# One fused attention and mixture-of-experts kernel: the routing arithmetic and the shared expert reordered at the seam between its two halves

## Chip, core and metric

The kernel runs on one core of a Trainium2 chip (trn2). Its time is device time in microseconds, the median over runs. Five engines work side by side, each in its own program order: PE (TensorE) multiplies matrices, DVE (VectorE) and ACT (ScalarE) do elementwise work, POOL (GpSimd) does elementwise work and issues indirect DMAs, and SP (SyncE) issues the plain DMAs. They meet only at semaphores that the program sets and waits for.

## What is computed

A layer in two halves, on 2048 tokens of width 512. The first half is cross attention with 16 heads whose queries, keys, values and probabilities are rounded to 8 bits. The second is a mixture of experts:

```python
logits = flat @ router_w.T                        # flat: layernorm of x, 2048 x 512; 32 experts
scores = sqrt(softplus(logits))
_, idx = top_k(scores + expert_bias, 4)
topv = take_along_axis(scores, idx, axis=1)
topv = topv / (topv.sum(-1, keepdims=True) + 1e-20)
out = sum over experts of p[:, None] * clamped_swiglu(flat, wg, wu, wd)   # p is topv, zero elsewhere
out = out + clamped_swiglu(flat, shared_gate_w, shared_up_w, shared_down_w)
return x + out                                    # x already holds the attention's result
```

`clamped_swiglu` clips both products to -7..7, takes `silu(g) * u` (256 wide) and multiplies by the down weights. The shared expert serves every token; a routed expert serves only those tokens that chose it.

## The kernel before

Tokens go in 16 tiles of 128 (`TT = 16`, numbered from 0), heads in 16 units a tile, so attention has 256 units (`LAST` is unit 255). A unit's scores go from PSUM to SBUF on DVE, through the exponential on ACT, through a DMA transpose on SP, are widened from uint8 to bf16 on POOL (`probs_ready`) and are multiplied by the values on PE (`av_done`). When all units of a tile are done, DVE normalises it (`an`, L643 and L648), PE projects it, and `x1`, `xn2` (its layernorm) and the router's logits follow. `LAG = 7` is the distance in units at which PE follows. Unit 254 is an exception: DVE widens it (`widen`, L1104 to L1109), so that POOL has only unit 255 left.

The seam is what comes after unit 255 and before the first routed tile. Each engine has a program for it: `pe_early`, `act_early`, `dve_early`, `pool_early` and `sp_early`. All but the last begin with a loop over `l` in 0..31, which plays out the last steps of the attention with the seam's work put at chosen values of `l`. Three chains run there.

- **Routing** (mostly DVE). `soft_first` and `soft_last` make the softplus with ACT's Exp and Ln; ACT's Sqrt gives the scores; `choose_first` and `choose_last` find the best four and write one-hot masks (`maskb`, `r_mask`); `pe_ranks` counts by matmuls how many earlier tokens chose each expert (`r_totals`); from that DVE works out each token's slot (`base`, `slotf`, `slot_n`) and builds, for each of the four choices `j`, the operands of a matmul that makes the token list: `name_of(j, 0)`, `name_of(j, 1)` and `place_of(j)`. PE multiplies them (`pe_list(j)`, `listed`). After the fourth DVE writes `rows_sb` (`rows_ready`), and POOL gathers the first tokens with it. The routing is done for tiles 0 to 12 first (`TA = 13`, the slice `most`), then for tiles 13 to 15 (`rest`).
- **Shares.** The normalised weight of each chosen expert is written to DRAM beside the token (`share_ready`, then one DMA on SP).
- **Shared expert**, 16 tiles. ACT does Silu (`act_silu`), DVE multiplies (`hidden(k)`, L926, `h_ready`), PE transposes (`pe_hidden`), ACT evacuates (`act_hidden`), PE does the down product (`pe_down`), ACT evacuates into one of four buffers `y` (`act_early_out`), and POOL adds it to the output with an indirect DMA (`add`, L1309), whose landing frees the buffer. Gate and up products of tiles 0 to 12 (`GATED = 13`) were made during the attention and lie in DRAM; four buffers `xg` take them back. SP loads them (`tokens(k)`, which waits until `hidden(k - 4)` has freed the buffer), and tile 4 to 12 are clamped on POOL (L1369), in program order ahead of `add(k - 6)`. `gate(k)` clamps tiles 13, 14 and 15 out of PSUM on DVE; `pe_up` makes them.

SP also loads the first five routed experts (`load_expert`, two pieces of 768 KB each; `FREE_RING = 5`) while the shared expert runs: both pieces of expert 0 right after `tokens(8)`, of expert 1 after `tokens(9)`, and so on to `tokens(12)`; then it stores the shares. Experts 5, 6 and 7 are loaded when `listed` says that the list is made.

The routed stage follows: 78 tiles, each with gathers on POOL and two products and a transpose on PE. It is not touched by the change.

## Time and profile before

| | us |
|---|---|
| median of 3 runs | 1362.32 |
| lowest and highest run | 1361.37 and 1363.89 |
| the profiled execution's own time | 1359.23 |
| its span (first to last instruction) | 1357.5 |
| PE busy in the span | 1189.9 |
| DVE busy in the span | 1106.5 |
| attention's last exponential starts (from the span's start) | 819.31 |
| first gather of routed tokens is issued | 907.64 |
| first product of the routed stage | 917.6 |

Times below count from the start of the span. A row of the timeline gives start, duration, engine, line, operation, output and input, shape and count, and in brackets how long the engine had been idle before it and what released it. Several instructions of one line are merged into one row.

### The profile page before, as it was taken

What the parts mean: (1) busy time and instruction counts of PE and PEld (TensorE: products, weight loads), DVE (VectorE), ACT (ScalarE), POOL (GpSimd) and SP (SyncE); (2) the same over time, 40 slices, a digit from 0 to 9 for tenths busy, and PEclk for the clock granted to TensorE, in tenths of its full rate; (3) what the DMA queues carried; (4) which work ended last, traced back from release to release, by engine and by line L of the source; (5) the groups of instructions that cost most, each with busy time, mean ns of one, the idle gap of its engine ahead of it and who ended that gap; (6) DMA issues with size and microseconds to landing.
All of it is one profiled execution on the core that took longest, in us unless ns stands there. A gap on an engine that the chain in (4) does not pass through costs nothing.

```text
span 1357.5 us, 29324 instructions
## 1 busy us (share of the span) xinstructions
PE 1189.9 (88%) x7425; PEld 594.4 (44%) x7523; DVE 1106.5 (82%) x2287; ACT 938.2 (69%) x1345; POOL 886.3 (65%) x905
## 2 busy tenths in 40 slices
PE   7999577888888889888888886759999999999995
PEld 3444134444444455444444443324444444444442
DVE  4557899999999999999999998865767767766663
ACT  2224398999999999999999996424555555555552
POOL 3222388998889898989889985374445445445443
PEclk9999789999999999999999997989999999999997
DMA  7565877787777677776767794896778887786542
GB/s 264 134 155 132 162 133 159 138 162 139 143 148 154 141 148 142 148 150 144 151 138 146 143 211 100 269 219 180 159 207 224 221 231 190 182 236 176 91 69 26
DMA packets 400754, 219.32 MB, mean 162 GB/s; under 512 B 357287, under 2 KB 357415, under 8 KB 400690
## 3 DMA queue, kind: packets, MB, share of 16 engines
q1 hardware_dynamic: 380354, 179.72, 55.4%
q0 software_dynamic: 20336, 38.83, 16.0%
q8 instruction: 29, 0.48, 0.1%
q14 instruction: 35, 0.29, 0.1%
HBM read 101.10 MB, written 40.89 MB: 105 GB/s over the span
## 4 chain that ended last, share of the span: by engine, by line
PE 49%; issue 18%; DVE 17%; POOL 5%; ACT 5%; DMA 4%; SPq 1%; DVEq 0%; POOLq 0%; ACTq 0%; another core or an unknown queue 0%
PE psS L1417 20%; PE psS L885 10%; DVE mem L638 6%; DVE mem L654 6%; PE psS L477 4%; POOL mem L728 3%; ACT mem L595 3%; PE psS L1864 3%; DMA mem<-mem 2%; PE psAV L1851 2%; PE psP L864 1%; PE psAV L528 1%; PE psP L427 1%; POOL mem L711 1%; PE psAV L448 1%
## 5 line engine op out<-in xcount | busy, mean ns | idle before, releaser
L595 ACT ACTIVATE mem<-mem 128x2048 uint8<-128x2048 f32 x256 | 534.0, 2087 | 32.3 <-POOL mem L711 27.9
L728 POOL TENSOR_SCALAR mem<-mem 128x2048 bf16<-128x2048 uint8 x255 | 484.1, 1898 | 30.5 <-DMA mem<-mem 10.6
L477 PE MATMUL psS<-mem 128*128 128x512 bf16 x928 | 290.6, 387 | 88.2 <-DVE mem L654 37.7
L654 DVE TENSOR_SCALAR_CACHE_REDUCE mem<-psS,mem 128x1024 f32<-128x1024 f32 x256 | 327.6, 1280 | 3.0 <-PE psS L477 2.9
L638 DVE TENSOR_SCALAR_CACHE_REDUCE mem<-psS 128x1024 f32<-128x1024 f32 x256 | 312.5, 1221 | 13.1 <-PE psS L477 10.6
L1417 PE MATMUL psS<-mem 128*128 x624 | 295.2, 596 | 0.0
L1309 POOL DMA_INDIRECT out_y<-mem x78 | 123.9, 1588 | 192.1 <-DVE mem L1494 96.5
L885 PE MATMUL psS<-mem 128*128 (+1 forms) x376 | 180.6, 603 | 10.0 <-ACT mem L899 10.0
L502 PEld LDWEIGHTS psAV<-mem 128*128 128x128 bf16 x4096 | 138.6, 96 | 91.7 <-issue 22.8
L477 PEld LDWEIGHTS psS<-mem 128*128 128x128 bf16 x1024 | 72.2, 98 | 218.6 <-DVE mem L638 124.9
L502 PE MATMUL psAV<-mem 128*128 128x32 bf16 x4096 | 142.3, 177 | 26.5 <-ACT mem L568 14.6
L1417 PEld LDWEIGHTS psS<-mem 128*128 128x128 f32 x624 | 112.2, 191 | 114.1 <-issue 113.6
L920 DVE TENSOR_SCALAR mem<-psS 128x512 f32<-128x512 f32 x78 | 53.9, 692 | 123.2 <-PE psS L1417 123.2
L1506 DVE STREAM_TRANSPOSE mem<-mem 64x256 f32<-64x256 f32 x312 | 136.2, 437 | 4.5
L1460 ACT ACTIVATE mem<-mem 32x256 f32<-32x256 f32 x308 | 127.5, 414 | 8.0
L1304 POOL DMA_INDIRECT mem<-xn_dram,mem x85 | 88.6, 1043 | 39.0 <-issue 24.6
L885 PEld LDWEIGHTS psS<-mem 128*128 128x128 f32 x376 | 71.0, 192 | 94.9 <-issue 84.4
L913 ACT ACTIVATE mem<-mem 128x256 f32<-128x256 f32 x94 | 38.9, 416 | 84.7 <-DVE mem L920 81.1
L899 ACT ACTIVATE mem<-psP 128x256 f32<-128x256 f32 x78 | 29.9, 383 | 93.9 <-PE psP L864 93.9
L711 POOL TENSOR_SCALAR mem<-mem 128x1 f32<-128x1 f32 x256 | 68.3, 267 | 38.9 <-DVE mem L654 14.5
L448 PE MATMUL psAV<-mem 128*128 128x512 f32 x128 | 65.1, 593 | 0.0
L427 PE MATMUL psP<-mem 128*128 128x512 f32 x120 | 62.8, 605 | 0.0
(229 smaller groups left out, 1313.6 us busy)
## 6 DMA issues: line engine op xcount, KB each, us to landing
mem<-in_moe_w SPq DMA_DIRECT2D x64, 768.0 KB, 6.5
xn_dram<-mem SPq DMA_DIRECT2D x29, 256.0 KB, 2.3
mem<-in_x SPq DMA_DIRECT2D x28, 256.0 KB, 3.0
mem<-mem SPq DMA_TRANSPOSE x292, 3.1
mem<-in_ctx_in SPq DMA_DIRECT2D x16, 256.0 KB, 3.6
mem<-xn_dram SPq DMA_DIRECT2D x16, 256.0 KB, 3.0
out_y<-mem SPq DMA_DIRECT2D x16, 256.0 KB, 2.2
gated_dram<-mem SPq DMA_DIRECT2D x13, 256.0 KB, 2.2
```

Source lines behind the costliest of these rows:

```text
L477: last = nc.tensor.matmul(psS[c][:, k * D:(k + 1) * D], qT[pm][:, hm, :], kT[:, hm, c * HALF + k * D:c * HALF + (k + 1) * D], start=True, ...
L502: last = nc.tensor.matmul(bank[:, ho * HD:(ho + 1) * HD], pb[slot][:, b // 2, b % 2, :], v[:, b, ho * HD:(ho + 1) * HD], start=(b == 0), s ...
L595: nc.scalar.activation(p8[slot], S[slot], ACT.Exp, bias=NB[:, slot:slot + 1], scale=sq[p][:, h:h + 1], accum_out=Z[p][:, h:h + 1]).then_in ...
L638: nc.vector.tensor_scalar(S[slot][:, 0:HALF], psS[0][:], 1.0, None, ALU.mult, ALU.max, accum_out=M[:, 2 * slot:2 * slot + 1]).then_inc(hal ...
L654: nc.vector.tensor_scalar(S[before][:, HALF:TK], psS[1][:], 1.0, M[:, 2 * before:2 * before + 1], ALU.mult, ALU.max, accum_out=M[:, 2 * be ...
L728: nc.gpsimd.tensor_scalar(pb[slot], pT[slot].bitcast(U8).rearrange("p (j q b) -> p j b q", b=2, q=P), 1.0, 0.0, ALU.mult, ALU.add).then_in ...
L885: last = nc.tensor.matmul(bankY[o], hT[o][:, c, :], w(DC * 2 * I + c * D, D), start=(c == 0), stop=(c == I // P - 1))
L1304: nc.gpsimd.indirect_dma_start(out=xg[l], out_offset=None, in_=xn2_dram, in_offset=bass.IndirectOffsetOnAxis(list_column, 0), bounds_check ...
L1309: nc.gpsimd.indirect_dma_start(out=out, out_offset=bass.IndirectOffsetOnAxis(out_rows, 0), in_=values, in_offset=None, compute_op=ALU.add, ...
L1417: last = nc.tensor.matmul(bankG[o], stationary[:, c, :], w(c * 2 * I, 2 * I), start=(c == 0), stop=(c == DC - 1))
L1460: nc.scalar.activation(whole[to, :, 1 - j::2, :], blocks[i][of, :, j::2, :], ACT.Copy).then_inc(xT_ready if last else placed, 1)
L1506: last = nc.vector.transpose(blocks[i][64 * g:64 * g + 64, :, 2 * h:2 * h + 2, :].rearrange("p c t b -> p c (t b)"), xg[l][rows_in, 0:D].r ...
```

## The change

DVE's order is changed most. At `l == 0` only two operations of the softplus for tiles 0 to 12 stay (`soft_open`, the two that ACT's Ln waits for), directly followed by `widen`; the other four (`soft_rest`), `soft_last`, `gate(13)`, `hidden(0)` and `hidden(1)` move behind the step `l == LAG`, whose end normalises attention tile 15. `hidden(2)` and `hidden(3)`, until now inside `choose_last`, move out: to the front of the second softplus, and behind the second mask. The shares are made for tiles 0 to 12 right after their mask and for 13 to 15 after theirs. All later `hidden` calls come two numbers lower in the same places, and the fourth list gets two of its own (14 and 15). PE's rank products are split: all that needs only the masks of tiles 0 to 12 comes before `pe_hidden(1)` and `pe_down(0)`, and the rest, six small products, after them. `pe_list` 0, 1, 2, 3 now stand after the down products of tiles 10, 12, 14 and 15. ACT's Sqrt for tiles 0 to 12 moves to `l == LAG`, and its Silu and evacuation of the first shared tiles move back. SP puts one piece of an expert between `tokens(8)` to `tokens(11)`, so two experts in all, then waits for both shares, stores them, and loads the other three experts (six pieces).

The core of the diff:

```diff
 # pe_early
-                if l == LAG:
-                    for c in range(2):
-                        pe.wait_ge(half_max[c], TT * H)
-                    pe_hidden(pe, 0, 0)
                 if l == 14:
                     pe_up(pe, GATED + 1)
                 if l == 28:
-                    pe_hidden(pe, 1, 1)
+                    for c in range(2):
+                        pe.wait_ge(half_max[c], TT * H)
+                    pe_hidden(pe, 0, 0)
             pe_up(pe, GATED + 2)
+            pe.wait_ge(x1_ready, TT)
+            pe.wait_ge(gu_ready, 2)
+            pe_ranks_first(pe)
+            pe_hidden(pe, 1, 1)
             pe.wait_ge(shared_in, 16 * SHARED_PIECES)
             pe_down(pe, 0, 0, shared_weights)
+            pe_ranks_last(pe)
             for k in range(2, SHARED):
...
-                if k == 2:
...
-                    pe_ranks(pe)
-                if k == 12:
+                if k == 11:
                     pe_list(pe, 0)
-                if k == 15:
+                if k == 13:
                     pe_list(pe, 1)
+            pe_list(pe, 2)
             pe_down(pe, SHARED - 1, (SHARED - 1) % 2, shared_weights)
             pe_experts(pe)
-            for j in range(2, TOP):
-                pe_list(pe, j)
+            pe_list(pe, 3)

+        def pe_ranks_last(pe):
+            pe.wait_ge(r_mask, 2)
+            nc.tensor.matmul(bankR[:, TA * E:TT * E], upper[:], maskb[:, TA * E:TT * E], start=False, stop=False)
+            for d in range(1, TT - TA):
+                nc.tensor.matmul(bankR[:, TA * E:TT * E], onesb[:], maskb[:, (TA - d) * E:(TT - d) * E],
+                                 start=False, stop=(d == TT - TA - 1))
+            for t in range(TA, TT):
+                last = nc.tensor.matmul(bankX[:, 0:E], onesb[:], maskb[:, t * E:(t + 1) * E],
+                                        start=False, stop=(t == TT - 1))

 # dve_early
                 if l == 0:
...
-                    soft_first(most, 1)
+                    soft_open(most, 1)
                     widen(LAST - 1)
+                if l == LAG:
+                    soft_rest(most)
+                    soft_last(most, 1)
                     gate(GATED)
-                    soft_last(most, 1)
                     hidden(0)
                     hidden(1)
-                if l == LAG:
                     choose_first(most, range(0, TA), 1)
-                    choose_last(most, range(0, TA), {1: 2, 2: 3})
+                    choose_last(most, range(0, TA), {})
+                    shares(most, range(0, TA))
...
                     gate(GATED + 1)
-            soft_first(rest, 2)
+            hidden(2)
+            soft_open(rest, 2)
+            soft_rest(rest)
             soft_last(rest, 2)
             gate(GATED + 2)
             choose_first(rest, range(TA, TT), 2)
             choose_last(rest, range(TA, TT), {})
             dve.wait_ge(r_mask, 2)
-            hidden(4)
...
-            hidden(5)
...
+            hidden(3)
+            shares(rest, range(TA, TT))
...
             for j in range(TOP):
                 name_of(j, 0)
-                if j < 3:
-                    hidden(10 + 2 * j)
+                hidden(8 + 2 * j)
                 name_of(j, 1)
-                if j < 3:
-                    hidden(11 + 2 * j)
+                hidden(9 + 2 * j)
                 place_of(j)

+            def shares(c, tiles):
+                then(v_.tensor_tensor(prod[:, c, :], score[:, c, :], full[:, c, :], ALU.mult))
+                then(v_.tensor_reduce(share_sum[:, c], prod[:, c, :], AX.X, ALU.add))
+                then(v_.tensor_scalar(share_sum[:, c], share_sum[:, c], 1e-20, None, ALU.add))
+                then(v_.reciprocal(share_sum[:, c], share_sum[:, c]))
+                v_.tensor_tensor(share[:, c, :], prod[:, c, :], ..., ALU.mult).then_inc(share_ready, 1)

 # sp_early
             for k in range(2 * MU, GATED):
                 tokens(k)
-                for piece in range(2):
-                    load_expert(sp, k - 2 * MU, k - 2 * MU, piece)
-            sp.wait_ge(share_ready, 1)
+                if k < 3 * MU:
+                    load_expert(sp, (k - 2 * MU) // 2, (k - 2 * MU) // 2, k % 2)
+            sp.wait_ge(share_ready, 2)
             sp.dma_start(xn2_dram[:, D:D + E].rearrange("(t p) e -> p t e", p=P), share).then_inc(share_stored, 16)
+            for e in range(MU // 2, FREE_RING):
+                for piece in range(2):
+                    load_expert(sp, e, e, piece)
```

`act_early` moves the Sqrt of tiles 0 to 12 from `l == 1` to `l == LAG`, `act_silu(2)` to `l == 17`, `act_hidden(0)` to `l == 27`, and puts `act_silu(3)` and `act_hidden(1)` behind the second Sqrt.

## Rows read from the trace of the kernel before

**Rows 1.** The page's chain of work that ended last, share of the span by line.

```profile
PE psS L1417 20%; PE psS L885 10%; DVE mem L638 6%; DVE mem L654 6%; PE psS L477 4%; POOL mem L728 3%; ACT mem L595 3%; PE psS L1864 3%; DMA mem<-mem 2%; PE psAV L1851 2%; PE psP L864 1%; PE psAV L528 1%; PE psP L427 1%; POOL mem L711 1%; PE psAV L448 1%
```

**Rows 2.** The instructions of L1417, the routed products: ns min/median/max, starts.

```profile
L1417 PE MATMUL psS<-mem x624: 592/592/1062, 917.6 to 1335.3; 128*128 x156
```

**Rows 3.** The timeline of DVE, 819 to 831.

```profile
819.68 2.16 DVE L1065 TENSOR_TENSOR mem<-mem 128x416 f32<-128x416 f32 x1
...
825.70 2.83 DVE L1108 TENSOR_SCALAR mem<-mem 128x2048 bf16<-128x2048 uint8 x1
...
830.83 0.24 DVE L643 RECIPROCAL mem<-mem 128x16 f32<-128x16 f32 x1
```

**Rows 4.** The timeline of POOL, 819 to 828.

```profile
819.36 2.04 POOL L728 TENSOR_SCALAR mem<-mem 128x2048 bf16<-128x2048 uint8 x1
...
825.54 1.90 POOL L728 TENSOR_SCALAR mem<-mem 128x2048 bf16<-128x2048 uint8 x1 [1.81 <-DMA mem<-mem]
```

**Rows 5.** The timeline of SP's queue, the transpose of unit 254.

```profile
818.88 1.23 SPq L810 DMA_TRANSPOSE mem<-mem  x1
```

**Rows 6.** DMA issues between 817.5 and 820, last number us to landing.

```profile
mem<-mem SPq DMA_TRANSPOSE x1, 3.1
```

**Rows 7.** The timeline of DVE, 831 to 848.

```profile
831.72 0.58 DVE L1078 TENSOR_TENSOR mem<-mem,ebias_sb 128x416 f32<-128x416 f32 x1
...
844.40 0.55 DVE L926 TENSOR_TENSOR mem<-mem 128x256 f32<-128x256 f32 x1 [4.83 <-PE psS L864]
...
847.98 0.21 DVE L1062 TENSOR_SCALAR mem<-mem 128x96 f32<-128x96 f32 x1 [0.63 <-ACT mem L1028]
```

**Rows 8.** The timeline of DVE, 854 to 872.

```profile
854.75 0.50 DVE L1098 CAST mem<-mem 128x96 bf16<-128x96 f32 x1
...
855.62 0.69 DVE L1136 TENSOR_TENSOR mem<-mem 128x512 f32<-128x512 f32 x1
...
859.84 0.42 DVE L926 TENSOR_TENSOR mem<-mem 128x256 f32<-128x256 f32 x1 [2.81 <-PE psS L864]
...
861.63 0.19 DVE L1145 TENSOR_SCALAR mem<-psAV 128x32 f32<-128x32 f32 x1
...
871.42 2.59 DVE L1174 TENSOR_SCALAR mem<-count,mem 128x104 f16<-128x104 f32 x8
```

**Rows 9.** Waits between 855 and 905: us in total, times, longest.

```profile
ACT mem L999 <- DMA out_y<-mem,own_rows: 11.0, 5, 3.6
```

**Rows 10.** The timeline of PE, 855 to 915.

```profile
855.63 3.40 PE L972 MATMUL psAV<-mem,onesb 128*128 128x480 bf16 x15 [2.65 <-DVE mem L1098]
...
863.41 1.88 PE L885 MATMUL psS<-mem 128*128 128x512 f32 x4
...
879.06 3.43 PE L885 MATMUL psS<-mem 128*128 128x512 f32 x4 [3.75 <-ACT mem L899]
...
905.23 0.91 PE L991 MATMUL psAV<-mem 128*128 128x104 f16 x16 [3.53 <-DVE mem L1181]
914.81 1.12 PE L1407 MATMUL psT<-ident,mem 128*128 128x128 f32 x4 [8.68 <-DMA mem<-xn_dram,mem]
```

**Rows 11.** The timeline of DVE, 891 to 899.

```profile
891.11 2.40 DVE L1174 TENSOR_SCALAR mem<-count,mem 128x104 f16<-128x104 f32 x8 [0.42 <-PE psAV L991]
...
895.90 2.28 DVE L1181 TENSOR_TENSOR mem<-count_h,mem 128x2048 f16<-128x2048 f16 x1
```

**Rows 12.** The timeline of POOL, 896 to 908.

```profile
896.14 3.46 POOL L1309 DMA_INDIRECT out_y<-mem,own_rows  x1 [0.30 <-issue]
...
901.75 1.54 POOL L1309 DMA_INDIRECT out_y<-mem,own_rows  x1 [0.30 <-issue]
...
907.64 1.09 POOL L1304 DMA_INDIRECT mem<-xn_dram,mem  x1 [1.05 <-DVE mem L1200]
```

**Rows 13.** The timeline of ACT, evacuations of shared tiles 8 and 10.

```profile
881.46 0.60 ACT L999 ACTIVATE mem<-psS 128x512 f32<-128x512 f32 x1 [2.45 <-DMA out_y<-mem,own_rows]
...
890.58 0.60 ACT L999 ACTIVATE mem<-psS 128x512 f32<-128x512 f32 x1 [2.28 <-DMA out_y<-mem,own_rows]
```

More of the change, by code:

```diff
@@ L1015, in act_early @@
                         act_silu(act, k, k)
+                if l == LAG:
                     act.wait_ge(r_soft, 1)
                     nc.scalar.activation(first(score), first(full), ACT.Sqrt).then_inc(r_sqrt, 1)
-                if l == 4:
+                if l == 17:
+                    act_silu(act, 2, 0)
+                if l == 27:
                     act_hidden(act, 0, 0)
-                if l == 7:
-                    for k in range(2, 4):
-                        act_silu(act, k, k % 2)
-                if l == 27:
-                    act_hidden(act, 1, 1)
             act.wait_ge(logits_cp, TT)
@@ L1064, in soft_first, with soft_rest @@
                 then(v_.tensor_scalar(full[:, c, :], u[:, c, :], -1.0, None, ALU.add))
+            def soft_rest(c):
                 then(v_.tensor_tensor(prod[:, c, :], ex[:, c, :], full[:, c, :], ALU.subtract))
@@ L1068, in soft_first @@
                 then(v_.tensor_scalar(sel[:, c, :], logits[:, c, :], 0.0, None, ALU.max))
+            def shares(c, tiles):
[3 more added lines that the diff above has]
+                then(v_.reciprocal(share_sum[:, c], share_sum[:, c]))
+                v_.tensor_tensor(share[:, c, :], prod[:, c, :],
+                                 share_sum[:, c].unsqueeze(2).to_broadcast([P, len(tiles), E]),
+                                 ALU.mult).then_inc(share_ready, 1)
             def soft_last(c, turn):
@@ L1134, in dve_early @@
             dve.wait_ge(r_mask, 2)
-            hidden(4)
-            then(v_.tensor_tensor(prod, score, full, ALU.mult))
-            then(v_.tensor_reduce(share_sum, prod, AX.X, ALU.add))
-            hidden(5)
-            then(v_.tensor_scalar(share_sum, share_sum, 1e-20, None, ALU.add))
-            then(v_.reciprocal(share_sum, share_sum))
-            v_.tensor_tensor(share, prod, share_sum.unsqueeze(2).to_broadcast([P, TT, E]), ALU.mult).then_inc(share_ready, 1)
+            hidden(3)
+            shares(rest, range(TA, TT))
             then(v_.memset(ones_e, 1.0))
@@ L1150, in dve_early @@
             then(v_.tensor_scalar(base, base, float(P), None, ALU.mult))
-            hidden(6)
+            hidden(4)
             then(v_.tensor_tensor(sel, bankR.rearrange("p (t e) -> p t e", t=TT),
@@ L1155, in dve_early @@
             then(v_.tensor_reduce(slotf[:, 0, :], prod, AX.X, ALU.add))
-            hidden(7)
+            hidden(5)
             then(v_.tensor_tensor(prod, onehot[1], sel, ALU.mult))
@@ L1159, in dve_early @@
             then(v_.tensor_tensor(prod, onehot[2], sel, ALU.mult))
-            hidden(8)
+            hidden(6)
             then(v_.tensor_reduce(slotf[:, 2, :], prod, AX.X, ALU.add))
@@ L1163, in dve_early @@
             then(v_.tensor_reduce(slotf[:, 3, :], prod, AX.X, ALU.add))
-            hidden(9)
+            hidden(7)
             then(v_.tensor_scalar(slot_n, slotf, 1.0 / P, -0.5 + 0.5 / P, ALU.mult, ALU.add))
```

37 lines of the change are left out of this document (21 added, 16 removed).

## The prediction

> **What bounds the kernel now.** I read the chain of waits first. The page's shares show the routed products of L1417 as its largest member, 20% [rows 1]; the seam's own lines are spread thin there. The routed stage starts at 917.6 and its products run from then on at one steady length [rows 2]. Nothing in the change touches it, so what the change is worth is how much earlier the first gather, now at 907.64 [rows 12], is issued. I then read the timelines of DVE, POOL and PE from the last attention units to that gather, and last the waits.
>
> Up to 855 DVE works nearly without pause. The pauses are 4.83 us before `hidden(3)`, which sits inside the choice of tiles 0 to 12 and waits for PE's transpose, and 0.63 us before the second softplus [rows 7]. Then come 2.81 us before `hidden(5)`, which again waits for PE: PE is busy with the rank products for 3.40 us, after 2.65 us of idleness [rows 8, 10]. From 871.42 on DVE builds the lists [rows 8]. There it depends on the shared expert, and that on DMAs: ACT waits 11.0 us, in five waits, for earlier outputs to land before it may reuse their buffers [rows 9].
>
> **The change, part by part.** I follow DVE, because every link up to the lists is its own.
>
> *Widening unit 254.* The softplus operations ahead of it (`soft_rest`) take 825.70 - 819.68 = 6.02 us [rows 3]. The unit's transpose is issued at 818.88 and lands 3.1 us later, at 821.98 [rows 5, 6], so `widen` can start at 822.0 and end at 824.9, 3.7 us sooner. Unit 255 is then the later one: POOL widens it from 825.54 to 827.44 [rows 4]. With half a microsecond for PE's product, DVE can normalise tile 15 at 828.1 where it now starts at 830.83 [rows 3]: 2.7 us sooner. Reciprocal and normalisation take 0.9 us (831.72 - 830.83, [rows 3, 7]), to 829.0. DVE idles twice for this, 2.3 us before `widen` and 3.2 us after it. That is as much as the 4.83 + 0.63 us that leave.
>
> *The moved block.* `soft_rest` now follows. Its first operation took 2.16 us while POOL was running its own widening until 821.40 [rows 3, 4]. In the new place POOL has only the small layernorm work of tile 14, so I take 0.6 us for it plus some overlap. The 128x416 addition of L1078 takes 0.58 us [rows 7]. Bounds of the block: 4.5 and 6.0 us; I take 4.7, to 833.7. `soft_last`, gate(13), `hidden(0)` and `hidden(1)` now fill 828.53 to 830.83, 2.3 us [rows 3]: to 836.0. The choice, the token numbers and gate(14) take 847.98 - 831.72 = 16.3 us, less 4.83 and 0.63 idle and 0.8 for two `hidden` that leave [rows 7], thus 10.0: to 846.0 without the shares, which come inside it. Shares for 13 of 16 tiles: all 16 now cost 861.63 - 855.62 = 6.0, less 2.81 idle and 0.5 for a `hidden` and a memset, 2.7 us [rows 8]; 2.4 for 13 of them (between 2.2 by size and 2.7). To 848.4. `hidden(2)` 0.35: 848.7. The second softplus and choice, 855.25 - 847.98 = 7.3 us [rows 7, 8]: mask complete at 856.0, against 855.25 now. `hidden(3)`, shares of three tiles and the memset, 1.8 us (small operations of 0.2 to 0.3 each, like the 0.21 us of L1062 [rows 7]): 857.8.
>
> *Rank products.* Only six small ones are left behind the last mask. Fifteen wide ones take 3.40 us at the lower clock [rows 10], so six of 96 columns or fewer cost at most their share of that, 1.4 us, and at least 0.3. Even 1.4 (857.4) is hidden by the 1.8 us on DVE. The first part needs gate(14), so it runs at 848.4 to 852.2, and `pe_down(0)` is done by 854.2: PE has slack. So DVE starts L1145 at 857.8 where it starts at 861.63 [rows 8]. Gain so far 3.8 us. From there to the first list DVE needs 871.42 - 861.63 = 9.8 us [rows 8], to 867.6, with `hidden` 4 to 7 where 6 to 9 are. These need one shared tile per 2.2 us or more, and PE makes one in 1.9 (one down product, [rows 10]).
>
> *The lists.* Two halves of names, two `hidden` and a place take 895.90 + 2.28 - 891.11 = 7.1 us [rows 11]; the first round has 0.4 more for the expert ends. `hidden` of the second half ends 4.8 us into its round, and PE then does a transpose, a down product of 1.88 and the list of 0.91 before DVE may refill the buffers [rows 10]: 3.0 us. So rounds 2 and 3 start 0.7 us late each. `hidden(11)` ends at 867.6 + 7.5 + 4.8 = 879.9, `hidden(13)` at 887.7, `hidden(15)` at 895.5. After that PE has in order a transpose, `pe_down(14)`, list 2, `pe_down(15)` and list 3: about 5.6 us (0.3 + 2 x 1.8 + 2 x 0.85, [rows 10]), to 901.1. Today list 3 waits only for DVE's last place and ends at 906.14 [rows 10]. This tail is a cost of the change, as are two `hidden`, but 5 us remain.
>
> *POOL.* Today the gather follows the list's end by 1.5 us [rows 10, 12]. In the new order `y(15)` is ready only at about 900.8, the adds go one behind another at 1.54 + 0.30 us [rows 12], and the one at 897 falls inside the last place. The add at 896.14 took 3.46 instead of 1.54 us: it began during the L1181 at 895.90 and lasted until 1.44 us past its end at 898.18 [rows 11, 12]. So I let the add of tile 13 wait for the place at 895.5 to 897.8, then three adds follow, the last when `y(15)` allows, from 901.4 to 903.2, and the gather starts at 903.5. Gain 4.1 us.
>
> On this the Trainium skill speaks (SBUF — State Buffer, section Who interferes with whom): it infers that a `tensor_tensor`, which L1181 is, takes only a read interface and leaves the writing of descriptors free. The rows show otherwise. By that rule the adds would leave POOL free and the gather would start 1.5 us after the list's end, at 902.6.
>
> *Token loads and the ring of `y`.* `hidden(4)` to `hidden(8)` come 1 to 4 us later than now, and the loads of tiles 8 to 12 with them. Between these SP now puts four pieces of expert weights instead of ten, so 1 MB goes per token tile instead of 1.8. The add of tile k - 4 must land before tile k is evacuated, and it stands on POOL behind the clamp of tile k + 2. Today that ring holds tile 8 until 881.46 and tile 10 until 890.58 [rows 13]. In the new order tile 8 must be evacuated by 879, or list 0, behind `pe_down(10)`, is late. I cost the loads at nothing, hidden by the bandwidth that six fewer pieces leave; what it costs without that cover is rival (d). The six pieces follow later, and no routed tile needs them before 917.
>
> *PE's clock.* After 2.65 us of idleness the rank products ran slow, and after 3.75 us a down product took 3.43 us instead of 1.88 [rows 10]. In the new order PE idles some 2.6 us before `hidden` 10, 12 and 14. Each time the clock falls there, the next list is 1.2 us later (1.55 less the 0.35 us of slack to the next `hidden`), and the rest with it. One such fall in three is my value, nothing and 3.6 us the bounds.
>
> *The gather's landing.* It lands 7.2 us after its issue (907.64 to PE's first transpose behind it at 914.81 [rows 10, 12]). The six pieces of experts 5 to 7 are issued when list 3 is done, and lead it by 2.4 us instead of 1.5; nothing to 0.9 us later, I take 0.3.
>
> Sum: 4.1 - 1.2 - 0.3 = 2.6 us off the profiled execution (1359.23, span 1357.5), so 1356.6. The median of the runs is 3.1 us above that execution; I take the same saving from it: 1362.3 - 2.6 = 1359.7.
>
> **Rivals.** (a) *The clock falls at all three gaps.* For it: 2.65 us was enough once. Against it: shorter pauses between the list rounds now leave the products alone. Gain 0.2: 1362.1. (b) *Place and add run side by side.* The last adds are not held, and the gather goes with the list, 0.9 us earlier (902.6). With no clock fall the gain is 5.0 - 0.3: 1357.6. Against it stands the add of 3.46 us [rows 12]; for it stands the Trainium skill's inference above. (c) *Given back in the ring of `y`.* The relief of the DMA is partly eaten by the later start; tile 8 is evacuated near 883, list 0 is 4 us late, and the gather goes where it goes today: 1362.3. (d) *Slower.* The ring turns no faster than now although it starts with `hidden(4)` 3.7 us later (859.0 against 855.3, [rows 8]). Tile 8 is evacuated at 885.2 and tile 10 at 894.3 [rows 13]. `pe_down(10)` then starts at 886.6 and list 0 ends at 889.3, against 882.9 in my own sum; the second wait adds 0.5. Gather at 910.4, 2.8 us later than today: 1365.1. It decides from tile 8 at 885 on. Against it: the bytes ahead of the token loads are nearly halved.
>
> **How the numbers follow.** A difference under 0.2% (2.7 us) can't be told from none on this kernel. My own case (one clock fall or none, gains 1.7 to 3.8) gets 0.42, and more than half of it lies over 2.7; its range is 1358.5 to 1360.6. (a) 0.18, (b) 0.10, (c) 0.19, (d) 0.11. Faster: 0.28 of my case, (b), and 0.02 of (c) and (a) where less is given back: 0.40. Same: the remainder, 0.49. Slower: 0.11. The range runs from 1357.6, (b), past (a) and (c), to 1363.3, 1 us beyond (c), and leaves (d) out.
>
> **What would show it.** Right: `widen` starting by 822.5 and the normalisation by 828.5; the second mask near 856.0; L1145 near 858; the first list near 867.6; tile 8 evacuated by 879; list 3 ending near 901 to 902.5, and the gather 1 to 2.5 us after that, behind the last add. Wrong: `soft_rest` held by POOL for 6 us; DVE waiting for Silu at `hidden` 10 to 12; PE at the lower clock in the list rounds; a first gather that takes longer to land because the loads of experts 5 to 7 lead it by more.

## The result and the profile after: the first gather goes 5.2 us later, not 4.1 us sooner

| | us |
|---|---|
| kernel before, median of 22 runs | 1363.05 (1359.58 to 1367.87) |
| changed kernel, median of 22 runs | 1367.74 (1361.31 to 1371.46) |
| ratio | 1.0028, 95% interval 1.0017 to 1.0039 |
| profiled execution of the changed kernel | 1368.61, span 1366.9 |

The change makes the kernel 0.28% slower by the ratio (3.8 us), 4.7 us by the medians. The two profiled executions differ by 9.4 us, twice as much: the one of before lies 3.8 us under its median, the one of after 0.9 us above. The part up to the seam, the same in all kernels of this document, takes a varying time from one execution to the next. So below I count from one instant that all kernels share, the start of DVE's four clamps of tiles 0 to 3 (815.3 in the profile of before, 815.39 in that of after, up to 820.6 elsewhere), and write +n for n us after it.

| | before | after |
|---|---|---|
| first operation on the rank totals | +46.3 | +43.8 |
| first list begins | +56.1 | +53.6 |
| first gather | +92.35 | +97.52 |
| first routed product | +102.30 | +109.86 |
| first to last routed product | 417.7 | 419.2 |

The routing is 2.5 us sooner, as meant. Then the stretch from the rank totals through the lists to the gather loses 7.7 us, the gather's landing 2.4 and the routed stage 1.5.

The timeline of DVE in the changed kernel up to the first list (line numbers are the changed kernel's):

```profile
822.58 2.50 DVE L1131 TENSOR_SCALAR mem<-mem 128x2048 bf16<-128x2048 uint8 x1 [2.35 <-DMA mem<-mem]
829.06 0.25 DVE L643 RECIPROCAL mem<-mem 128x16 f32<-128x16 f32 x1 [3.99 <-PE psAV L502]
...
829.96 0.99 DVE L1079 TENSOR_TENSOR mem<-mem 128x416 f32<-128x416 f32 x1
...
859.21 0.19 DVE L1167 TENSOR_SCALAR mem<-psAV 128x32 f32<-128x32 f32 x1
...
868.96 1.43 DVE L1196 TENSOR_SCALAR mem<-count,mem 128x104 f16<-128x104 f32 x4
```

`widen` starts on landing and takes 2.50 us; the normalisation follows at 829.06, `soft_rest` at 829.96, the second mask ends at 857.5, L1167 (L1145 before) starts at 859.21, the first list at 868.96. Compare [rows 3, 8].

The timeline of DVE in the changed kernel, last list rounds:

```profile
889.78 2.05 DVE L1196 TENSOR_SCALAR mem<-count,mem 128x104 f16<-128x104 f32 x8 [5.73 <-PE psAV L1003]
...
894.03 0.41 DVE L926 TENSOR_TENSOR mem<-mem 128x256 f32<-128x256 f32 x1
...
898.88 2.07 DVE L1196 TENSOR_SCALAR mem<-count,mem 128x104 f16<-128x104 f32 x8 [2.24 <-PE psAV L1003]
...
903.17 0.41 DVE L926 TENSOR_TENSOR mem<-mem 128x256 f32<-128x256 f32 x1
...
910.67 0.27 DVE L1219 TENSOR_SCALAR mem<-psAV 128x104 f32<-128x104 f32 x1 [4.89 <-PE psAV L1003]
```

Three pauses, of 5.73, 2.24 and 4.89 us, each ended by PE's L1003, the products of a list. In [rows 11] the pause at that place was 0.42 us. The timeline of PE in the same stretch:

```profile
885.31 3.48 PE L885 MATMUL psS<-mem 128*128 128x512 f32 x4 [2.40 <-ACT mem L899]
888.58 1.13 PE L1003 MATMUL psAV<-mem 128*128 128x104 f16 x16
...
892.50 3.57 PE L885 MATMUL psS<-mem 128*128 128x512 f32 x4
...
896.12 1.88 PE L885 MATMUL psS<-mem 128*128 128x512 f32 x4
...
901.62 2.53 PE L885 MATMUL psS<-mem 128*128 128x512 f32 x4
...
904.37 2.76 PE L885 MATMUL psS<-mem 128*128 128x512 f32 x4
...
909.72 0.91 PE L1003 MATMUL psAV<-mem 128*128 128x104 f16 x16
922.44 1.12 PE L1429 MATMUL psT<-ident,mem 128*128 128x128 f32 x4 [11.80 <-DMA mem<-xn_dram,mem]
```

Down products (L885) take 3.48, 3.57, 2.53 and 2.76 us; only those at 896.12 and 907.70 take 1.88 and 1.95. Against [rows 10] the slow length is now the usual one. The granted clock is 0.83 in each stretch of 10 us from 880 to 910 (before: 0.86, 1.00, 0.84), a mix of its two levels, 1.2 and 2.4 GHz; it fell after idle stretches of 2.40 to 2.60 us (2.51 and 2.60 stand before the transposes that lead the products at 892.50 and 901.62). The length of the pause alone does not decide it: in e7 below the clock fell after 1.69 us, in e6 it was still at the upper level in the product after 3.04 us. And list 0 at 888.58 stands behind a down product that waited for ACT. The timeline of ACT in the changed kernel, then POOL's, then the waits between 855 and 925 (us in total, times, longest):

```profile
881.50 0.60 ACT L1011 ACTIVATE mem<-psS 128x512 f32<-128x512 f32 x1 [0.84 <-DMA out_y<-mem,own_rows]
884.57 0.42 ACT L913 ACTIVATE mem<-mem 128x256 f32<-128x256 f32 x1 [2.47 <-POOL mem L1391]
884.89 0.37 ACT L899 ACTIVATE mem<-psS 128x256 f32<-128x256 f32 x1
...
893.58 0.60 ACT L1011 ACTIVATE mem<-psS 128x512 f32<-128x512 f32 x1 [7.26 <-DMA out_y<-mem,own_rows]
```
```profile
881.34 3.19 POOL L1391 TENSOR_SCALAR mem<-mem 128x512 f32<-128x512 f32 x1 [2.40 <-DMA mem<-gated_dram]
...
894.96 3.11 POOL L1331 DMA_INDIRECT out_y<-mem,own_rows  x1 [2.94 <-ACT mem L1011]
...
911.06 1.54 POOL L1331 DMA_INDIRECT out_y<-mem,own_rows  x1 [0.97 <-ACT mem L1011]
912.91 1.09 POOL L1326 DMA_INDIRECT mem<-xn_dram,mem  x1 [0.31 <-issue]
```
```profile
ACT mem L1011 <- DMA out_y<-mem,own_rows: 20.9, 7, 7.3
```

Backwards from list 0: `act_hidden(10)` (ACT, L899, 884.89) is behind Silu of tile 12 (L913), which waits for POOL's clamp of tile 12 (L1391, 881.34). That clamp waited 2.40 us for its token load, and then took 3.19 us where most of its neighbours take 0.60, ending 0.48 us after DVE's `place_of` of 881.78 to 884.05 ("place" below). ACT's waits for landings of the adds are 20.9 us in seven, against 11.0 us in five [rows 9]; the longest, 7.26 us, holds the evacuation of tile 10. The fences that follow show SP's queue in the changed kernel, then the windows of 890 to 900, first of the kernel before, then of the changed one (last three columns: granted clock, DMA share, GB/s), and then their DMA issues of 860 to 900 (number of adds, median us to landing) in the same order:

```profile
871.72 0.33 SPq L1239 DMA_DIRECT2D mem<-gated_dram  x1
...
872.58 8.49 SPq L1234 DMA_DIRECT2D mem<-in_moe_w  x1
```
```profile
core 0: us, PE busy (x) PEld busy (x) DVE busy (x) ACT busy (x) POOL busy (x), PEclk, DMA share, GB/s
...
890.00:900.00 10.00, 9.20 (x54) 4.74 (x53) 8.79 (x25) 4.80 (x11) 8.57 (x5) 1.00 0.90 124
```
```profile
890.00:900.00 10.00, 6.52 (x28) 3.16 (x28) 7.76 (x24) 2.95 (x7) 6.36 (x4) 0.83 1.08 292
```
```profile
out_y<-mem,own_rows POOLq DMA_INDIRECT x12, 6.0
```
```profile
out_y<-mem,own_rows POOLq DMA_INDIRECT x11, 8.2
```

The last token load leaves at 871.72 (868.31 before) and is used 9.6 us later; the six pieces follow from 872.58. In the kernel before the crowd of transfers is gone by 890 (124 GB/s after that); the changed kernel still moves 292 GB/s. An add lands after 8.2 us in the median instead of 6.0.

### The profile page after: what moved, and what is told of

Read it like the earlier page. It is cut to its first block, busy times and chain, and to the rows that moved or that the text cites. A ratio compares the mean times of both kernels' runs of the same rounds, so it can differ in the third digit from the quotient of the medians.

```text
span 1366.9 us, 29435 instructions
## 1 busy us (share of the span) xinstructions
PE 1209.7 (89%) x7526; PEld 595.2 (44%) x7527; DVE 1105.5 (81%) x2292; ACT 938.4 (69%) x1345; POOL 887.9 (65%) x905
## 4 chain that ended last, share of the span: by engine, by line
PE 50%; issue 18%; DVE 16%; POOL 6%; ACT 5%; DMA 4%; SPq 1%; POOLq 0%; DVEq 0%; ACTq 0%
PE psS L1439 20%; PE psS L885 12%; DVE mem L654 6%; DVE mem L638 5%; PE psS L477 4%; POOL mem L728 4%; ACT mem L595 3%; PE psS L1886 3%; DMA mem<-mem 2%; PE psAV L1873 2%; PE psAV L528 1%; PE psP L864 1%; PE psP L427 1%; POOL mem L711 1%; PE psAV L502 1%
## 5 line engine op out<-in xcount | busy, mean ns | idle before, releaser
L477 PE MATMUL psS<-mem 128*128 128x512 bf16 x1024 | 311.0, 386 | 73.2 <-DVE mem L638 32.1
L885 PE MATMUL psS<-mem 128*128 (+1 forms) x376 | 184.4, 614 | 5.8 <-ACT mem L899 5.8
L920 DVE TENSOR_SCALAR mem<-psS 128x512 f32<-128x512 f32 x78 | 53.9, 691 | 120.1 <-PE psS L1439 120.1
L885 PEld LDWEIGHTS psS<-mem 128*128 128x128 f32 x376 | 72.1, 196 | 91.2 <-issue 85.5
L913 ACT ACTIVATE mem<-mem 128x256 f32<-128x256 f32 x94 | 39.0, 416 | 82.3 <-DVE mem L920 74.7
L899 ACT ACTIVATE mem<-psP 128x256 f32<-128x256 f32 x78 | 30.0, 384 | 92.7 <-PE psP L864 89.6
```

The lines of the kernel that those rows point to most:

```text
L477: last = nc.tensor.matmul(psS[c][:, k * D:(k + 1) * D], qT[pm][:, hm, :], kT[:, hm, c * HALF + k * D:c * HALF + (k + 1) * D], start=True, ...
L885: last = nc.tensor.matmul(bankY[o], hT[o][:, c, :], w(DC * 2 * I + c * D, D), start=(c == 0), stop=(c == I // P - 1))
```

## Experiments

Thirteen kernels, each timed beside the kernel before. "Gather" is the first gather.

| | ratio to before (95%) | lists begin | gather | first routed product | routed stage |
|---|---|---|---|---|---|
| before | 1 | +56.1 | +92.35 | +102.30 | 417.7 |
| after | 1.0028 (1.0017 to 1.0039) | +53.6 | +97.52 | +109.86 | 419.2 |
| e1 | 1.0034 (1.0019 to 1.0048) | +53.8 | +94.57 | +108.11 | 419.3 |
| e2 | 1.0020 (1.0005 to 1.0036) | +57.4 | +95.98 | +105.72 | 417.2 |
| e3 | 1.0081 (1.0058 to 1.0103) | +53.9 | +102.65 | +114.35 | 419.5 |
| e4 | 1.0015 (0.9998 to 1.0033) | +56.5 | +94.59 | +104.93 | 418.1 |
| e5 | 0.9998 (0.9987 to 1.0008) | +53.8 | +92.33 | +100.63 | 421.1 |
| e6 | 0.9968 (0.9954 to 0.9983) | +57.0 | +94.79 | +101.14 | 417.7 |
| e7 | 0.9995 (0.9982 to 1.0008) | +52.7 | +97.47 | +105.14 | 417.2 |
| e8 | 1.0002 (0.9987 to 1.0018) | +53.1 | +93.33 | +101.12 | 422.2 |
| e9 | 1.0043 (1.0027 to 1.0059) | +53.3 | +90.34 | +96.78 | 433.3 |
| e10 | 1.0015 (0.9999 to 1.0032) | +53.5 | +94.42 | +106.84 | 417.8 |
| e12 | 1.0042 (1.0026 to 1.0057) | +53.6 | +85.79 | +91.70 | 435.9 |
| e13 | 0.9980 (0.9968 to 0.9992) | +53.8 | +90.42 | +96.46 | 424.5 |
| e14 | 0.9983 (0.9966 to 1.0000) | +53.7 | +91.18 | +97.23 | 425.9 |

The places are those of one execution each, the ratios those of many. Kernels with the same instructions up to the gather show how far a single place can be trusted: before and e6 differ by 0.9 us where the lists begin and by 2.4 us at the gather, after and e7 by 0.9 and 0.1. So a difference of up to some 2.5 us at the gather is not more than two executions of one kernel can show, and for the kernel's time I go by the ratio.

**The weights' traffic (e5, e3, e4).** e5 is the changed kernel with experts 2 to 7 loaded only after the first gathers have landed:

```diff
-            for e in range(MU // 2, FREE_RING):
-                for piece in range(2):
-                    load_expert(sp, e, e, piece)
...
             sp.wait_ge(listed, TOP)
-            for s in range(FREE_RING, RING):
+            sp.wait_ge(tokens_in[MU - 1], 16)
+            for s in range(MU // 2, RING):
```

> The changed kernel with less DMA work in the seam: experts 0 and 1 are loaded as there, but the six pieces of experts 2 to 4, and those of 5 to 7, are issued only when the first four gathers have landed. Nothing is left out. Theory B (burst): what made the changed kernel slow is that its six pieces are issued in one burst at 872.6 and stretch the landing of the clamped tokens and of the adds to 8.7 to 9.9 us just when list 0 depends on them. Then DVE's pauses of 5.73 and 2.24 us fall to about 1 each, adds land in 4 to 6 us, the gather is issued 5 to 7 us sooner against the last unit of attention, and it lands in 4 to 6 us instead of 9.5: 7 to 11 us faster than the changed kernel, 3 to 6 us under the kernel before. Theory O (order): the pauses come from PE's order of lists and down products, whatever the DMAs do; then only the landing gets shorter, 3 to 5 us under the changed kernel.

The timeline of DVE in e5, its three pauses:

```profile
889.46 2.13 DVE L1196 TENSOR_SCALAR mem<-count,mem 128x104 f16<-128x104 f32 x8 [1.71 <-PE psAV L1003]
...
898.54 2.05 DVE L1196 TENSOR_SCALAR mem<-count,mem 128x104 f16<-128x104 f32 x8 [2.07 <-PE psAV L1003]
...
908.96 0.27 DVE L1219 TENSOR_SCALAR mem<-psAV 128x104 f32<-128x104 f32 x1 [3.55 <-PE psAV L1003]
```

The pauses are 1.71, 2.07 and 3.55 us instead of 5.73, 2.24 and 4.89: 5.5 us less, and the gather goes 5.2 us sooner. So the six pieces between 872.58 and 900 are the largest cause of the late gather, and the gain in the routing was real. At list 0 it can be followed: tile 12's clamp ends 4.7 us sooner (+64.4 instead of +69.1), 2.2 us of it because its load lands sooner and 2.5 because the clamp then misses DVE's place and takes 0.66 us instead of 3.19. Yet the gather is only level with before's although the lists begin 2.3 us sooner: something else costs 2 us, as far as one execution tells.

The kernel's time is another matter. The median falls to 1362.72, level with before, but e5 also holds experts 5 to 7, and e7 below, which does only that and keeps the six pieces where they are, comes out the same (0.9995 against 0.9998). e5's first product is 4.5 us sooner than e7's, and its routed stage, which now gets experts 2 to 4 late, is 3.9 us longer. So no run shows that moving the burst alone shortens the kernel; that two such kernels come out alike within 1 us was what the expectation of e7 gave to its theory O, while the shorter pauses and the sooner gather speak for theory B.

e3 puts both pieces of an expert back after each `tokens(k)`, as before, in the changed kernel; e4 puts the changed SP order alone into the kernel before.

```diff
 # e3, in sp_early of the changed kernel
-                if k < 3 * MU:
-                    load_expert(sp, (k - 2 * MU) // 2, (k - 2 * MU) // 2, k % 2)
+                for piece in range(2):
+                    load_expert(sp, k - 2 * MU, k - 2 * MU, piece)
```

> The changed kernel with the loads of expert weights as in the kernel before: two pieces behind each of the token loads 8 to 12. Theory R: the ring of y and the clamps are slower still, tile 12 is clamped 4 us later than 881 to 884, list 0 ends 3 to 5 us later, and the kernel is 2 to 4 us slower than the changed one. Theory C or a cost in DVE's own order: no difference over 1 us.

> The kernel before with the changed order of SP's loads alone (one piece of an expert between tokens 8 to 11, then the shares, then six pieces). Theory R: ACT's waits for landed outputs shrink from 11 to under 6 us, DVE's pauses before hidden(11) to (13), 4.1 us in all, fall below 1.5, and the gather is issued 2 to 4 us sooner: 1 to 4 us faster than the kernel before. Theory that the relief is worth nothing, as adds land as late as before: within 1 us.

DVE's longest pause in e3, then the longest of ACT's waits in e4, from their timelines:

```profile
900.34 2.04 DVE L1196 TENSOR_SCALAR mem<-count,mem 128x104 f16<-128x104 f32 x8 [8.60 <-PE psAV L1003]
```
```profile
894.90 0.60 ACT L999 ACTIVATE mem<-psS 128x512 f32<-128x512 f32 x1 [7.38 <-DMA out_y<-mem,own_rows]
```

e3's ratio is another 0.0053 higher: the pause before the third list is 8.60 us. So four pieces between the token loads instead of ten are right once these are asked for later, as the prediction had it; it is the burst behind them that it missed. e4 was expected to gain 1 to 4 us and does not: its gather goes 2.2 us later than before's and 0.2 us sooner than e6's, and the ratio of 1.0015 has an interval that just reaches 1, so a cost isn't shown either. But the same wait appears: one evacuation waits 7.38 us for a landing, behind the burst. Both orders move ten pieces, 7.5 MB, among adds that must land; the new one moves the crowd to where the lists wait for it.

**TensorE's clock (e10).** Small products without use, into a bank that is free then, fill three of PE's idle stretches:

```diff
                 pe_hidden(pe, k, k % 2)
+                if k == 11:
+                    fill(6)
                 pe_down(pe, k - 1, (k - 1) % 2, shared_weights)
...
                     pe_list(pe, 0)
+                    fill(8)
...
                     pe_list(pe, 1)
+                    fill(8)
# fill(n): n x nc.tensor.matmul(psT[:], onesb[:], maskb[:, 0:D], start=True, stop=True)
```

> The changed kernel with extra products on PE (22 of 128x512, their result unused, into a bank that is free then): 6 between the transpose of tile 11 and the down product of tile 10, 8 behind list 0, 8 behind list 1, where PE otherwise idles 2.4 to 2.6 us and its granted clock fell. In the changed kernel the down products of tiles 10, 11, 13 and 14 took 3.48, 3.57, 2.53 and 2.76 us instead of 1.9 to 2.0. Theory C (clock): they fall to 1.9 to 2.0, list 0's pause of 5.73 us shrinks by 1 to 1.5, the later ones by 1 to 3 in all, and the gather is issued 2 to 4.5 us sooner: 1 to 4 us faster than the changed kernel. Theory B (DMA alone): the clock recovers but tiles and adds come no sooner, so less than 1 us is won; and where the idle gap is shorter than the filling the kernel loses up to 1 us.

The timeline of PE in e10, down products of the list rounds:

```profile
886.52 1.98 PE L885 MATMUL psS<-mem 128*128 128x512 f32 x4 [0.62 <-ACT mem L899]
...
895.84 1.99 PE L885 MATMUL psS<-mem 128*128 128x512 f32 x4 [1.32 <-ACT mem L899]
...
901.30 1.88 PE L885 MATMUL psS<-mem 128*128 128x512 f32 x4
```

All down products from 886.52 on are back to 1.88 to 1.99 us (the one at 878.19, ahead of the first filling, took 3.12); granted clock 1.00 from 890 on. The pauses are 4.01, 2.37 and 3.56 us, 2.9 less in all, and the gather is 3.1 us sooner than after's: in these traces the clock is worth about 3 us of the 7.7, not all. That is little more than two executions can differ by, and in time it isn't shown: the ratio is 0.0013 lower (median 1365.41), and the two intervals overlap.

**The order of lists and down products (e1, e8).** e1 puts lists 0 to 2 ahead of the down product of their round instead of behind it (`if k in (11, 13, 15): pe_list(pe, (k - 11) // 2)` right after `pe_hidden`); e8 is e1 with e5's loads.

> The changed kernel, but lists 0, 1 and 2 stand right behind the transposes of tiles 11, 13 and 15, ahead of the down products of tiles 10, 12 and 14, so that they need nothing from the shared expert but DVE's own products. Theory R (ring): in the changed kernel list 0 waited on PE for pe_down(10), that for ACT's evacuation of tile 10, and that, in ACT's order, for tile 12's clamp on POOL. If so, DVE's 5.73 us pause before round 2 of the names falls to under 1.5, the 2.24 us before round 3 too, though hidden(12) may now itself wait for Silu; the gather is issued some 4 to 6 us earlier than in the changed kernel, and the time is 1 to 3 us under it (2 to 4 us above the kernel before at most). Theory C (PE's lower clock in the list rounds): the pauses stay above 3 us, since the products are as slow as before, and the time is unchanged within 1 us.

> Both edits on the changed kernel: lists 0 to 2 ahead of the down products, and experts 2 to 7 only after the first gathers. Theory B: with adds and tokens landing in time the order matters little, 0 to 2 us better than e5 (the tail behind hidden(15) is one down product shorter for list 3's readiness only, the adds stay). Theory O: 3 us or more better than e5.

The timelines of DVE (last place, reading of the list) and of POOL (last adds, first gather) in e8:

```profile
898.05 2.27 DVE L1200 TENSOR_TENSOR mem<-count_h,mem 128x2048 f16<-128x2048 f16 x1
904.26 0.27 DVE L1216 TENSOR_SCALAR mem<-psAV 128x104 f32<-128x104 f32 x1 [3.94 <-PE psAV L1000]
```
```profile
897.56 4.19 POOL L1326 DMA_INDIRECT out_y<-mem,own_rows  x1 [0.30 <-issue]
...
909.45 1.54 POOL L1326 DMA_INDIRECT out_y<-mem,own_rows  x1 [0.30 <-issue]
911.29 1.09 POOL L1321 DMA_INDIRECT mem<-xn_dram,mem  x1 [0.30 <-issue]
```

e1 brings the gather 3.0 us forward (4 to 6 were expected), but the first routed product follows 13.54 us behind it and the ratio is no better than after's. e8 tells more: its last place starts at +80.1, 7.5 us sooner than in the kernel before, and the list is read at 904.26. But the gather goes at 911.29, directly behind six adds with 0.30 us between them. POOL's train of adds is the next limit. It explains only part of the 2 us left by e5: there the list is read at 908.96, 0.8 us sooner than before's by the shared instant, and the adds take that up (last one at 909.35, gather at 911.20). The other 1.6 us went between the first list and that reading, where e5 has two `hidden` more (0.7 us) and down products of 3.54, 2.56 and 2.73 us. In time e8 is level with e5, as expected there if the order matters little.

**The gather's landing (e6, e7).** Loads of experts 5 to 7 wait until the fourth gather has landed: in the kernel before (e6) and in the changed one (e7). One line, `sp.wait_ge(tokens_in[MU - 1], 16)`, behind `sp.wait_ge(listed, TOP)`.

> The kernel before, with experts 5, 6 and 7 loaded only when the first four gathers have landed, instead of as soon as the list is made. Theory G: the first gathers share the DMA engines with these 4.7 MB; alone they land in 4 to 5 us instead of 7.2, so 2 to 3 us faster than the kernel before. Rival: the gathers' time is their own and the routed experts come late instead: no change or slower.

> The changed kernel with the same edit: experts 5, 6 and 7 wait for the first four gathers. The gather is issued as late as in the changed kernel (97.5 us after the clamps of tiles 0 to 3 begin, within 1), but lands in 4 to 6 us instead of 9.5: 3 to 5 us faster than the changed kernel. If theory B is right this is worth less than e5 by the 5 us that the burst costs; by theory O the two come out alike within 1 us.

The timeline of PE in e7, the first routed transpose:

```profile
919.45 1.12 PE L1430 MATMUL psT<-ident,mem 128*128 128x128 f32 x4 [7.16 <-DMA mem<-xn_dram,mem]
```

From gather to first product 9.95 us become 6.35 (e6), and 12.34 become 7.67 (e7), with no lengthening of the routed stage. PE's pause is 7.16 us instead of 11.80. e7's ratio is 0.0033 lower than the changed kernel's, and e6 beats the kernel before by 0.32%: at 1358.93 us it is the best of all. e7 is still 2.9 us above e6 by the medians, so with the loads held in both, the change stays the slower one.

The wait for the gather also reaches into the routed stage, by the clock: over its first 10 us the granted clock is 0.86 in the kernel before and 0.76 in the changed one, 0.90 in e6 and 0.91 in e7. As an estimate from these means, 10 us at 0.76 instead of 0.86 do 1.0 us less work, most of the 1.5 us that the changed kernel's routed stage is longer.

**Only the widening moved (e2).** The kernel before, with `widen(LAST - 1)` placed behind the second operation of `soft_first`.

> The kernel before with one part of the change alone: unit 254 is widened behind the first two softplus operations; the other four stay at l == 0 behind it. If early widening is worth what the changed trace shows for tile 15 (normalisation 1.8 to 2.7 us sooner), nothing is gained here, because DVE still does the four operations before it normalises: normalisation at the same time within 0.5 us, but PE's two last products some 2 us sooner. Theory R: time within 1 us of the kernel before. A rival, that PE's lower clock behind its last attention products is what costs, would show L442 at full clock and 1 us of gain.

The totals come at +47.4, 1.0 us later than in the kernel before, and the ratio is 1.0020. The early widening alone brings nothing: DVE idles 2.37 us for the landing ahead of it, and it takes 2.48 us itself.

**The tail (e9, e12, e13, e14).** e9: e1, e7's hold, list 3 ahead of `pe_down(15)`, and the first gathers ahead of the adds of tiles 12 to 15. e12: the same with e5's loads. e13: e9 with POOL's wait for all stored shared tiles moved from the start of `pool_routed` to its first routed add, and experts 5 to 7 held until they are stored. e14: e13 with `fill(6)` ahead of the transposes of tiles 10, 12 and 14.

```diff
 # e9, pool_early
             for k in range(SHARED):
...
+                if k == SHARED - MU:
+                    pool_first(pool)
                 add(k)
-            pool_first(pool)
```

> The changed kernel with its tail put in another order, and experts 5 to 7 held until the first four gathers have landed: lists 0, 1, 2 ahead of the down products of tiles 10, 12, 14; list 3 ahead of the down product of tile 15; on POOL the first four gathers ahead of the adds of tiles 12 to 15. The runs so far say that with the lists ahead POOL's train of adds is what holds the gather (last add 91.5 us after the clamps of tiles 0 to 3 begin, gather 93.3, rows ready near 86.5). Theory P (POOL's train and PE's tail): the gather is issued 86 to 90 us after those clamps instead of 97.5, lands in 6 to 8 us, and the kernel takes 1352 to 1357 us, 2 to 7 under the kernel before with held experts. Rival: the six pieces of experts 2 to 4 still stretch tokens and adds, the pauses before lists come back at hidden(12) to (14), and it is no faster than 1359.

> As e9, but the pieces of experts 2 to 4 too wait for the first gathers. Theory P: the gather is issued 84 to 87 us after the clamps; but as in e5 and e8 the routed stage loses 3 to 5 us to the late weights (its products lasted 421 to 422 us from first to last there instead of 417 to 419), so it ends within 2 us of e9.

The timelines of POOL and of PE in e9, last add before the pause and what follows it:

```profile
918.39 1.55 POOL L1329 DMA_INDIRECT out_y<-mem,own_rows  x1 [0.30 <-issue]
933.97 1.08 POOL L1324 DMA_INDIRECT mem<-xn_dram,mem  x1 [14.03 <-issue]
```
```profile
938.87 0.69 PE L864 MATMUL psP<-ident,mem 128*128 128x128 f32 x2 [12.31 <-DVE mem L926]
```

> This is e9 (lists as soon as their hidden tile is there, the first gathers ahead of the shared adds of tiles 12 to 15, experts 5 to 7 loaded behind the first gathers) with two changes: POOL waits for the 16 stored shared tiles only ahead of its first routed add, not ahead of its gathers, and the loads of experts 5 to 7 start only once all 16 shared tiles are stored. Theory (the 14.0 us pause of POOL in e9, put behind the stored tiles, is what made e9's routed stage 433.3 us long instead of 417.7): gather 88 to 91 us after the start of the clamps, landing in 4 to 6 us, first routed product at +95 to +98, no pause of POOL over 4 us behind it, routed stage 417 to 421 us, median 1354 to 1359. Rival (the added traffic of the adds simply moves into the routed stage, whose gathers or experts then come late): routed stage 424 us or more, median 1361 or more.

> As e13, with six small idle products ahead of the down products of tiles 10, 12 and 14. If the lower granted clock of the down products still costs something once the lists run early: the down products 1.9 us instead of 2.5 to 3.5, list rounds 1 to 2 us sooner, median 1 to 2 us below e13. If the list rounds are bound by the sums on DVE alone: within 0.5 us of e13, or up to 0.5 us above it.

The timeline of POOL in e13, the first gather behind the last shared add, and the longest wait:

```profile
923.70 1.08 POOL L1326 DMA_INDIRECT mem<-xn_dram,mem  x1 [0.30 <-issue]
...
942.88 1.61 POOL L1331 DMA_INDIRECT out_y<-mem  x1 [6.86 <-DMA out_y<-mem]
```

e9's routed stage starts 5.5 us sooner than before's and e12's 10.6 us sooner, and both are slower in the end (e9 1368.63 us, where 1352 to 1357 were expected). e12 without the burst is again no faster than e9 with it. POOL stands 14.03 us before its next gathers (933.97), waiting for the four last adds to land, and PE 12.31 us behind it. e13 removes exactly that (the gather follows at 923.70 with 0.30 us), and the ratio falls from 1.0043 to 0.9980. It also holds experts 5 to 7 longer, which no run tries by itself, but the pause of 14.03 us is gone, so the wait was the main cause. The expected 1354 to 1359 us are missed at 1361.20, and the rival foreseen there came in: the routed stage is still 424.5 us, with POOL waiting 6.86 us for a landing at 942.88, and PE 3.88 us. Which transfer is late there I did not try. The trace accounts for most of the 6.8 us over before's: PE's 3.88 us, the product behind that pause (945.42) of 3.47 us instead of 1.88, and a granted clock of 0.76 instead of 0.86 over the first 10 us. e14 is the same within its interval, but it asks little: in e13's list rounds only two down products are slow (2.58 and 3.78 us), and e14 still has one of 3.50. So what the clock costs with the lists ahead stays untold.

## Why the prediction was wrong, step by step

*Widening and normalisation: right.* Forecast 822.0 and 828.1, measured 822.58 and 829.06. `widen` took 2.5 us; e4 shows that it can take 1.23 when it starts first (below).

*The moved block: right.* 4.84 us (829.96 to 834.80) for a forecast of 4.7.

*Up to the rank totals: right in size.* Second mask 857.5 for 856.0, L1167 859.21 for 857.8, first list 868.96 for 867.6. Of the 3.8 us gain 2.5 are there. Of the 1.4 us missing, 1.0 is there when tile 15 is normalised: `widen` ended 0.2 us after its forecast, but unit 255, on landing, was widened on POOL from 826.46 where I had kept 825.54. The other 0.4 is in the choice and shares. The rank products were hidden, at 857.57 to 857.9.

*The lists: the first step that failed.* I had `hidden(11)`, (13) and (15) at 879.9, 887.7 and 895.5; they ended at 881.9, 894.4 and 903.6. So 2.0, 6.7 and 8.1 us late, in two jumps: 4.8 us at list 0 and 1.3 at list 1. My round was DVE's own work plus 0.7 us of PE.

*"Token loads and the ring of `y`": cost nothing. This is the wrong term.* I asked for tile 8 to be evacuated by 879, and it was at 881.50. I let the six pieces "follow later", since no routed tile needs them before 917, and did not ask what they stand in front of: the adds and the last token load, whose landings list 0 waits for by way of clamp, Silu and `act_hidden(10)`. e5 puts this at 5.2 us of the gather; in the old order (e4) no cost is clear of what two executions differ by. With the lists ahead of the down products, so that list 0 no longer waits for that chain, the same hold is worth only 1.2 us (e8 against e1).

*PE's clock: mechanism right, size wrong.* I took one fall in three, 1.2 us, with 3.6 as the bound; it fell three times, the first ahead of `pe_down(10)` and not of `hidden(10)`, and e10 gives 3.1 us back at the gather. [Rows 10] had shown it after 2.65 and 3.75 us (granted clock 0.50 over the 3.40 us of rank products), and after 2.40 to 2.60 us it fell again. The two terms overlap: idleness of PE comes from late tokens too.

*The tail and POOL: right in kind.* After `hidden(15)` I had 5.6 us to the end of list 3; it took 7.05, with the slow down product at 904.37. One add was held by a place, as forecast, 3.11 us; in e1 and e8 they take up to 4.64. The inference of the Trainium skill (SBUF — State Buffer, Who interferes with whom) that such an operation leaves descriptor writing free is not what these rows show. They show the hold and not its reason: an add also reads its row numbers from SBUF, and no run separates the two. The clamp of 3.19 us in the second round was a hold by that round's place, which I had not counted.

*The gather's landing: too small.* 0.3 us of at most 0.9 forecast, 2.4 measured. The loads of experts 5 to 7 are the larger part: holding them takes 4.7 us from it in e7 and 3.6 in e6. What leaves 1.3 us between e7 and e6 is not shown.

*The rivals.* (a) was right about the clock and (d) about the sign. Its figures were close (`pe_down(10)` at 886.6, list 0 ending 889.3, gather 910.4; measured 885.31, 889.7 and 912.91), but its path was not: tile 8 left at 881.50, before its limit of 885, and it was the token load of tile 12 with POOL's clamp that held `pe_down(10)`, and then the clock that held list 0. (b) and (c) did not happen. I gave (d) 0.11 on the ground that fewer bytes lie ahead of the token loads; that counted bytes ahead of one kind of transfer and forgot the rest.

What stays open: how the 4.7 us of the medians divide among these terms, since their places come from single executions, and which transfer makes POOL and PE wait in e13's routed stage.

## What to carry to other kernels

When loads are moved later because their own user is late, list every small transfer that is issued while they run and who waits for its landing: here adds and a token load of 256 KB among pieces of 768 KB held a chain that never reads the weights. Before moving a step forward, ask whether the whole chain to the next stage follows. Here 2.5 us gained in the routing met a shared expert that could not go faster, and the stronger lever was one wait: letting the first gathers land before the next weights are asked for saved 4 us in the kernel before.

## What the runs showed of the hardware

- DVE's widening of 128x2048 uint8 takes 1.23 us or twice that and more, and in these traces it went by which engine began first. In the changed kernel it starts at 822.58 while POOL widens, and ends 1.08 us after POOL does at 824.00; in e4 it starts 0.1 us before POOL's, takes 1.23, and POOL's takes 2.89 instead of about 1.9. The timelines of DVE and POOL in e4:

```profile
831.40 1.23 DVE L1108 TENSOR_SCALAR mem<-mem 128x2048 bf16<-128x2048 uint8 x1
```
```profile
827.55 1.89 POOL L728 TENSOR_SCALAR mem<-mem 128x2048 bf16<-128x2048 uint8 x1
831.50 2.89 POOL L728 TENSOR_SCALAR mem<-mem 128x2048 bf16<-128x2048 uint8 x1 [2.05 <-DMA mem<-mem]
```

- An add or a clamp on POOL that meets a place on DVE (L1203, a comparison of 128x2048 f16) can be held until 0.5 to 2.1 us after it: 3.11, 4.19 and 4.64 us (e8, 876.07) for an add instead of 1.54, and 3.19 for a clamp instead of 0.60. It isn't so each time: the clamp of 3.19 us began 0.44 us ahead of the place, the add of 4.19 us in e8 0.49 us ahead, but in the kernel before an add at 888.13, 0.27 us ahead of the place at 888.40, took 1.77 us.
- The indirect gather of 128 rows lands in 3.6 us in e9, 7.1 in the kernel before and 9.6 in e10. e6 shows what the plain loads do to it: the kernel before with these held back goes from the gather's issue to PE's first transpose in 3.6 us instead of 7.2.
- TensorE's clock is not told by the length of the pause alone: the next product of 128x512 took 3.14 us after 1.69 us of idleness in e7, and 1.98 us after 3.04 us in e6.
